# Softmax row inverses spread through DRAM instead of by GpSimd and TensorE, in the attention stage of a fused transformer layer

## The reference

```
n = (x - mean_c) / sqrt(var_c + 1e-6)                 # over channels
q, k, v = Wq n + bq, Wk n + bk, Wv n + bv             # 8 heads of 64
attn = softmax(q^T k / 8)                             # 1024 x 1024 per head
x = x + Wo (attn v) + bo
t = tokens(x);  n2 = layernorm(t)
aff = softmax(n2 gate) over 16 experts;  each expert takes its best 128 tokens of each image
t[index] += aff * (gelu(n2[index] w1 + b1) w2 + b2)
```

## Time and profile before

| | |
|---|---|
| median of 3 runs | 3368.14 us |
| range of the runs | 3366.99 to 3368.26 us |
| profiled execution, first to last instruction | 3365.4 us |
| what lies around that span | not given for the profiled execution; the median is 2.7 us above the span |
| mean granted TensorE clock | 0.976 of full speed |
| busy: PE, PEld, DVE, ACT, POOL | 3156.5, 2702.6, 2319.6, 1998.9, 1293.8 us |
| attention stage | up to about 2495 us of the span |

### The profile page before, as it was taken

How to read it: one execution, slowest core, us unless ns; L and a number is a source line. 1 busy time by engine, 2 the same in 40 slices (tenths; PEclk the granted TensorE clock), 3 DMA queues, 4 the chain that set the end, 5 groups by cost and what they waited for, 6 DMA issues and landing times. The chain is left out here.

```text
span 3365.4 us, 56592 instructions
## 1 busy us (share of the span) xinstructions
PE 3156.5 (94%) x18562; PEld 2702.6 (80%) x18562; DVE 2319.6 (69%) x3649; ACT 1998.9 (59%) x3833; POOL 1293.8 (38%) x1536
## 2 busy tenths in 40 slices
PE   6999999999999999999999999999954999999998
PEld 5988888788878887887888788888843888888886
DVE  5877587678768775875787687767756556555553
ACT  4876678478748856884787488568821333333332
POOL 1335234424523352344235233523432444444443
PEclk9999999999999999999999999999976999999999
DMA  6012111310220131113102201311132566655664
GB/s 219 26 51 104 49 51 39 113 53 26 81 97 26 51 109 45 51 40 112 53 26 95 84 26 51 113 28 37 39 114 52 139 125 139 139 135 122 150 135 59
DMA packets 108960, 269.39 MB, mean 80 GB/s; under 512 B 13456, under 2 KB 21648, under 8 KB 97936
## 3 DMA queue, kind: packets, MB, share of 16 engines
q1 hardware_dynamic: 80016, 198.80, 17.6%
q0 software_dynamic: 28672, 67.13, 11.3%
HBM read 158.40 MB, written 73.92 MB: 69 GB/s over the span
## 5 line engine op out<-in xcount | busy, mean ns | idle before, releaser
L728 DVE TENSOR_TENSOR PT<-ring,PT 128x512 fp32r<-128x512 f32 x1024 | 674.9, 686 | 226.5 <-ACT PT L476 220.1
L670 DVE TENSOR_REDUCE nmax<-S 128x1 f32<-128x1024 f32 x512 | 620.2, 1211 | 97.1 <-PE S L835 80.6
L878 PE MATMUL O<-PT,V 128*128 128x256 f32 x4096 | 677.1, 290 | 0.0
L396 POOL TENSOR_SCALAR rinv_bc<-ones,rinv 128x128 f32<-128x128 f32 x512 | 302.8, 603 | 950.3 <-DVE rinv L736 950.0
L846 PE MATMUL ring<-ident,prob 128*128 128x128 f32 x4096 | 623.3, 276 | 31.6 <-DVE qs L663 17.6
L476 ACT ACTIVATE PT<-ring 128x512 fp32r<-128x512 f32 x1024 | 581.6, 597 | 92.5 <-PE ring L846 79.8
L835 PE MATMUL S<-kd,qs 128*128 128x512 f32 x2048 | 600.2, 417 | 20.4 <-issue 17.9
L467 ACT ACTIVATE prob<-S,nmax 128x1024 f32<-128x1024 f32 x512 | 571.7, 1117 | 66.2 <-DVE nmax L670 66.2
L878 PEld LDWEIGHTS O<-PT,V 128*128 128x128 f32 x4096 | 577.4, 189 | 39.0
L846 PEld LDWEIGHTS ring<-ident,prob 128*128 128x128 f32 x4096 | 467.5, 141 | 72.0 <-DVE PT L728 31.6
L835 PEld LDWEIGHTS S<-kd,qs 128*128 128x128 f32 x2048 | 352.3, 191 | 72.6 <-issue 20.8
(11 more groups left out here) (115 smaller groups left out, 3721.1 us busy)
## 6 DMA issues: line engine op xcount, KB each, us to landing
kd<-kd SPq DMA_DIRECT2D x128, 256.0 KB, 3.6
wraw<-w_dram SPq DMA_DIRECT2D x32, 1024.0 KB, 6.7
wqk<-wqk_split SPq DMA_DIRECT2D x24, 1024.0 KB, 4.8
xt<-x_dram SPq DMA_DIRECT2D x16, 1024.0 KB, 7.2
PT<-wv_split SPq DMA_DIRECT2D x7, 2048.0 KB, 8.5
oT<-x_dram SPq DMA_DIRECT2D x24, 512.0 KB, 3.6
out_dram<-oT SPq DMA_DIRECT2D x48, 256.0 KB, 8.0
n_rows<-oT SPq DMA_DIRECT2D x48, 256.0 KB, 2.4
```

Of the source, the lines that this page charges most:

```text
L396: last_bc = nc.gpsimd.tensor_scalar(rinv_bc[:, k % 2, j, :], ones[:, :], rinv[:, 2 * k + j:2 * k + j + 1], None, ALU.mult)
L670: nc.vector.tensor_reduce(nmax[:, s:s + 1], S[:, s % 2, :], AX.X, ALU.max, negate=True).then_inc(max_done, 1)
L728: nc.vector.tensor_tensor(PT[:, 1, here[0], here[1], here[2]], ring[:, k % 2, :].rearrange("p (m q) -> p m q", m=4), PT[:, 0, here[0], her ...
L878: last_mm = nc.tensor.matmul(O[:, m % 2, 0:QC], V[:, t, head // 2, 2 * (head % 2):2 * (head % 2) + 2, :].rearrange("p h d -> p (h d)"), PT ...
```

## The change

The inverse row sums no longer go through POOL and PE. SP writes the 256 inverses of a block as one row into a DRAM tensor (from a [128 partitions x 2] tile, element by element), waits for that DMA, and loads the row back, broadcast over the 64 partitions of the head, into one of four slots of `Rs`. POOL multiplies by it as before. ACT copies the whole 128-partition product in one instruction into `oHL`; POOL now copies the other half across partitions (`oS2`) before it adds. pv_done comes from the last product. The K copies and weight loads are placed between the spreads. The residual of tiles 6 and 7 is loaded after block 2 and gets its bias at block 5, the other tiles in blocks 26 to 29, so nothing of `add_bo` is left after the last block. `ones` shrinks to one column, `n2T` moves into `Rs`.

```diff
+RES_TILES = {5: [6, 7], 26: [0], 27: [1, 2], 28: [3, 4], 29: [5]}
...
+    rinv_rows = nc.dram_tensor("rinv_rows", [BLOCKS, QC], F32).ap()
...
-        tmp = sb("tmp", [P, 3, 2, QC])
...
+        Rs = sb("Rs", [P, 4, QC])
+        oHL = sb("oHL", [P, 2, QC])
+        oS2 = sb("oS2", [P, 2, QC])
...
@@ sync
-                for p in range(1, PAIRS):
-                    duplicate_k(b, p)
-                    if p < PAIRS - 1 or not last:
-                        sp.wait_ge(ring_filled, b * RING + ring_proj(p, 3) + 1)
-                        load_pair(p % (PAIRS - 1) + 1)
...
-                for k in range(2):
+                def load_residual(k):
+                    if k == 3:
+                        sp.dma_start(spare[:, :, :], src[:, 6:8, :]).then_inc(res_in[k], 16)
+                        return
                     sp.wait_ge(os_lo, b * PIECES + 2 * k + 2)
-                    sp.dma_start(dst[:, k, :, :], src[:, 2 * k:2 * k + 2, :]).then_inc(res_in[0], 16)
...
+                    sp.sem_inc(sp_passed, 1)
+                    sp.dma_start(dst[:, k, :, :], src[:, 2 * k:2 * k + 2, :]).then_inc(res_in[k], 16)
+
+                def spread_inverse(m):
+                    row = rinv_rows[m:m + 1, :]
+                    odd = m // QB % 2
+                    sp.wait_ge(rinv_done, b * BLOCKS + m + 1)
+                    sp.dma_start(row.rearrange("a (u p) -> p (a u)", p=P), rinv[:, 2 * m:2 * m + 2],
+                                 allow_slow_non_contiguous=True).then_inc(rinv_out, 16)
+                    sp.wait_ge(rinv_out, b * (16 * BLOCKS) + 16 * m + 16)
+                    sp.sem_inc(sp_passed, 1)
+                    if m >= 4:
+                        sp.wait_ge(o_norm, b * BLOCKS + m - 3)
+                    sp.dma_start(Rs[D * odd:D * odd + D, m % 4, :], row.broadcast_to([D, QC])
+                                 ).then_inc(Rs_in[m % 4], 16)
+
+                for m in range(BLOCKS):
+                    if m % NT == NT - 1 and m < BLOCKS - 1:
+                        p = m // NT + 1
+                        duplicate_k(b, p)
+                        if p < PAIRS - 1 or not last:
+                            sp.wait_ge(ring_filled, b * RING + ring_proj(p, 3) + 1)
+                            load_pair(p % (PAIRS - 1) + 1)
+                    spread_inverse(m)
+                    if m == 2:
+                        load_residual(3)
+                    if m in (26, 27, 29):
+                        load_residual((26, 27, 29).index(m))
...
@@ gpsimd
-                        for j in range(2):
-                            last_bc = nc.gpsimd.tensor_scalar(rinv_bc[:, k % 2, j, :], ones[:, :],
-                                                              rinv[:, 2 * k + j:2 * k + j + 1], None, ALU.mult)
-                        last_bc.then_inc(rbc_done, 1)
...
-                        if BLOCKS - 2 <= k < BLOCKS:
-                            for i in range(2):
-                                add_bo(2 * (k - BLOCKS + 2) + i)
-                for i in range(4, NT):
-                    add_bo(i)
...
+                for m in range(BLOCKS):
+                    pair, odd, q = m // NT, m // QB % 2, m % QB
+                    rows, other = slice(D * odd, D * odd + D), slice(D * (1 - odd), D * (1 - odd) + D)
...
+                    for i in RES_TILES.get(m, []):
+                        add_bo(i)
...
+                    pool.wait_ge(o_copied, b * BLOCKS + m + 1)
+                    pool.sem_inc(pool_passed, 1)
+                    nc.gpsimd.tensor_copy(oS2[rows, m % 2, :], oHL[other, m % 2, :]).then_inc(o_shift, 1)
+                    pool.wait_ge(o_shift, b * BLOCKS + m + 1)
+                    nc.gpsimd.tensor_tensor(oHL[rows, m % 2, :], oHL[rows, m % 2, :], oS2[rows, m % 2, :],
+                                            ALU.add).then_inc(o_sum, 1)
+                    pool.wait_ge(o_sum, b * BLOCKS + m + 1)
+                    pool.wait_ge(Rs_in[m % 4], b * (4 * BLOCKS) + 16 * (m // 4) + 16)
+                    nc.gpsimd.tensor_tensor(oT[rows, pair, q * QC:(q + 1) * QC], oHL[rows, m % 2, :],
+                                            Rs[rows, m % 4, :], ALU.mult).then_inc(o_norm, 1)
...
@@ scalar, copy_output
-                    nc.scalar.activation(Rs[rows, m % 2, :], O[rows, m % 2, QC:2 * QC], ACT.Copy)
-                    nc.scalar.activation(oH[rows, m % 2, :], O[rows, m % 2, 0:QC], ACT.Copy)
-                    nc.scalar.activation(oL[rows, m % 2, :], O[other, m % 2, 0:QC], ACT.Copy).then_inc(o_copied, 1)
+                    nc.scalar.activation(oHL[:, m % 2, :], O[:, m % 2, 0:QC], ACT.Copy).then_inc(o_copied, 1)
...
@@ vector, tile_t
-                    dve.wait_ge(xbo, b * NT + i + 1)
+                    dve.wait_ge(xbo, b * NT + (2 if i >= 6 else i + 3))
...
@@ tensor
-                        last_mm.then_inc(pv_read, 1)
-
-                def inverse_sums(m):
-
-                    pe.wait_ge(rbc_done, b * BLOCKS + m + 1)
-                    for j in range(2):
-                        last_t = nc.tensor.transpose(O[:, m % 2, QC + j * P:QC + (j + 1) * P],
-                                                     rinv_bc[:, m % 2, j, :], ident)
-                    last_t.then_inc(pv_done, 1)
+                        last_mm.then_inc(pv_done, 1)
```

More of the change, by code:

```diff
@@ L120, in attention @@
         affT = oT[0:E, KC - 1, :]
-        tmp = sb("tmp", [P, 3, 2, QC])
[L122 to L126, removed]
+        Rs = sb("Rs", [P, 4, QC])
+        oHL = sb("oHL", [P, 2, QC])
+        oS2 = sb("oS2", [P, 2, QC])
+        n2T = Rs[:, :, :].rearrange("p (a b) c -> p a (b c)", a=2).rearrange("p a (k t) -> p a k t", k=KC)
         bv_bc = sb("bv_bc", [P, C])
@@ L133, in attention @@
         rinv = sb("rinv", [P, UNITS])
-        ones = sb("ones", [P, P])
-        rinv_bc = sb("rinv_bc", [P, 2, 2, P])
+        ones = sb("ones", [P, 1])
         stats = sb("stats", [P, 2, NT, 6])
@@ L168, in attention @@
         x_in = [sem(f"x_in{i}") for i in range(2)]
-        res_in = [sem(f"res_in{i}") for i in range(2)]
+        res_in = [sem(f"res_in{i}") for i in range(4)]
+        rinv_out = sem("rinv_out")
+        Rs_in = [sem(f"Rs_in{i}") for i in range(4)]
         wv_in = sem("wv_in")
@@ L196, in attention @@
         rinv_done = sem("rinv_done")
-        rbc_done = sem("rbc_done")
-        pv_read = sem("pv_read")
         pv_done = sem("pv_done")
         o_copied = sem("o_copied")
+        o_shift = sem("o_shift")
         o_sum = sem("o_sum")
@@ L382, in add_bo @@
                 def add_bo(i):
-                    if i % 4 == 0:
-                        pool.wait_ge(res_in[i // 4], b * 32 + 32)
+                    pool.wait_ge(res_in[i // 2], b * 16 + 16)
                     nc.gpsimd.tensor_tensor(res(i), res(i), bo_bc[:, :], ALU.add).then_inc(xbo, 1)
[L387 to L393, removed]
-                        pool.sem_inc(pool_passed, 1)
-                        for j in range(2):
-                            last_bc = nc.gpsimd.tensor_scalar(rinv_bc[:, k % 2, j, :], ones[:, :],
-                                                              rinv[:, 2 * k + j:2 * k + j + 1], None, ALU.mult)
-                        last_bc.then_inc(rbc_done, 1)
[L399 to L420, removed]
-                        if BLOCKS - 2 <= k < BLOCKS:
-                            for i in range(2):
-                                add_bo(2 * (k - BLOCKS + 2) + i)
@@ L424, in image, with tiles_added, pieces_split @@
-                for i in range(4, NT):
-                    add_bo(i)
+                def tiles_added(m):
+                    return sum(len(v) for k, v in RES_TILES.items() if k <= m)
+                def pieces_split(m):
+                    return sum(k - 2 < m for k in EARLY_BLOCK) + max(0, m - (BLOCKS - QB))
+                for m in range(BLOCKS):
+                    pair, odd, q = m // NT, m // QB % 2, m % QB
+                    rows, other = slice(D * odd, D * odd + D), slice(D * (1 - odd), D * (1 - odd) + D)
+                    if m:
+                        pool.wait_ge(o_norm, b * BLOCKS + m)
+                        pool.sem_inc(pool_passed, 1)
+                    for i in RES_TILES.get(m, []):
+                        add_bo(i)
+                    if m in RES_TILES:
+                        pool.wait_ge(xbo, b * NT + tiles_added(m))
+                        pool.sem_inc(pool_passed, 1)
+                    if pieces_split(m):
+                        pool.wait_ge(os_lo, b * PIECES + pieces_split(m))
+                        pool.sem_inc(pool_passed, 1)
+                    pool.wait_ge(o_copied, b * BLOCKS + m + 1)
+                    pool.sem_inc(pool_passed, 1)
+                    nc.gpsimd.tensor_copy(oS2[rows, m % 2, :], oHL[other, m % 2, :]).then_inc(o_shift, 1)
[6 more added lines that the diff above has]
+                                            Rs[rows, m % 4, :], ALU.mult).then_inc(o_norm, 1)
+                    for j in range(EARLY):
```

(9 more changed lines are left out.)

8 lines of the change are left out of this document (removed).

## The result

| | before | after |
|---|---|---|
| median of the runs | 3368.20 us (4 runs, 3366.99 to 3368.76) | 4386.78 us (4 runs, 4379.89 to 4393.22) |
| profiled execution, its span | 3365.4 us | 4393.22 us, span 4391.4 us |
| mean granted TensorE clock | 0.976 | 0.861 |

The ratio is 1.302 (95% interval 1.3007 to 1.3038): 1019 us slower, where 99 us faster was forecast. The range of 3225 to 3335 doesn't hold it.

The account below looks back on a forecast made before the run. The prediction took a normal block (5.68 us) to be bound by PE's rate alone. Inverse transposes 51, ACT copies 20 and residual 28 us made 99 us off 3368, so 3269 us, range 3225 to 3335.

Parts of the forecast that it names:

- SP and the DMAs at nothing: SP's write and read of the inverses: 3.0 us of SP a block, landing after 5.2, so costing nothing.
- the point that decides: In rival A: time from reciprocal to landing, r = 6.4 us, from which late inverses decide the kernel's time.
- rival A: DRAM round trip of the inverses too slow: at r = 8, 134 us more, 3403 us; chance 0.08.
- the cover: Inverses needed at POOL's product 13.2 us after their reciprocal; landing after 5.2 leaves 8 us of cover.
- Inverse transposes off PE: PE, 29 of 32 blocks: 0.22 us less each, block 5.47 us, 51 us over 8 images.
- Two ACT copies: ACT's output copies: two of three dropped, 0.68 us a block, worth 20 us (12.8 to 31.6), in the last pair.
- the chain there: Last pair, ACT to DVE to PE's next transpose: block falls from 6.14 to 5.46 us, just reaching PE's rate.
- Residual into the last pair: Wrap between images: normalisations of x no longer slowed by POOL's additions, 3.5 us a wrap, 28 us in all.
- POOL: nothing: POOL's new copy taken at 0.74 us, 2.2 us a block in all, plus late additions: costs nothing.
- B: Another chain between PE, ACT and DVE holds the block at 5.68 us: 3320 us; chance 0.12.
- C: PE not at its rate, 0.34 us a block hidden waiting: block 5.09 us, kernel 3183 us; chance 0.05.
- D: POOL's additions or the end of the last pair keep 3 to 5 us an image: about 3304 us; chance 0.15.

Follow-up runs that it names:

- probe: Separate program, no computation: SP issues seven forms of DMA one at a time; the change's write of 256 4-byte elements takes 8.35 us.
- probe2: Separate program, no computation, six forms differing in piece size, spacing or target: 256 4-byte pieces take 7.83 us adjacent, 1.57 us 64 bytes apart.
- k_on_act: Changed kernel with the K copies of pairs 1 to 3 issued by ACT instead of SP: 4216.81 us.
- old_spread: Changed kernel with the inverses again over POOL and PE; one ACT copy, POOL's shift and early residual stay: 3317.10 us, ratio 0.9845 to the kernel before.
- no_spread: Changed kernel without its two DMAs per block, the output multiplied by a tile of ones instead of the inverses: 3260.31 us.
- pair8: Changed kernel with each partition writing its two inverses as one 8-byte piece, POOL reading with a step of two: 3275.51 us, ratio 0.9724 to the kernel before.
- pipe: Changed kernel, 4-byte writes kept, SP issuing the write of a block before the read of the block before it: 3367.19 us.

## Why the prediction was wrong

**The failed step: SP and the DMAs at nothing.** The text read: "None in the trace writes single elements. The nearest for size is `affinities`, 64 KB in 2.2 us". It took 2.2, so 3.0 us of SP a block, "because most blocks have no large load in front of them". Measured: 9.6 us of SP a block, 8.2 of them at the wait for the write. The 9.1 us of the earlier trace rows was named as the upper end and comes close to the right price, though by chance: it belongs to a load of 2 KB behind large loads. It was given only to blocks with a large load ahead; `probe` shows 8.35 with nothing else running. The two rows said something of size and nothing of form. With 2.2 and 9.1 as ends and the point that decides, 6.4, between them, both sides of it needed a large chance. The Trainium skill (DMA: Bandwidth & Descriptors, Rules for kernel authors) was quoted in rival A against this write, as a non-contiguous last dim that becomes one descriptor per element. The warning pointed to the right DMA, and the packet counts agree with one descriptor per piece; but their number isn't the price, since 256 separate elements take 1.57 us in `probe2` when each has 64 bytes of its own.

**Rival A was the mechanism, with a chance of 0.08 and too small a price.** SP does one spread at a time, lags behind by 7 x (9.6 - 5.45) = 29 us in a pair, and the cover is used up. The rival had one r for two things, SP's time for a spread (9.6) and the time from reciprocal to landing (9.1 and a read of 3.9, 13 us). Even with r at 9.6 its sum gives 28.9 + 9.6 - 13.2 - 8.3 = 17 us a pair and 544 us in all, half of what was lost. Its sum let "8.3 of that" be absorbed before ACT's copy, for 134 us at r = 8. But the K copies stand in the same queue and have no such cover: PE needs them for the next pair's first scores. The prediction named that ("SP is also the queue for the K copies") and priced it for a spread of 3 us only. At 9.6 us the lag and the last spread come to 38 us, and 33 of them land on PE at each of 24 boundaries, 799 in all; the last blocks of the image and the wraps have 293 of the other 330, and there the lag of the last pair is the likely reason. `k_on_act` shows that it isn't the K queue alone: without it the inverses themselves stop ACT and PE, and 957 us are left.

**Inverse transposes off PE: right.** The block became 5.45 (forecast 5.47), PE without a wait in it. 57 us between `old_spread` and `no_spread` against 51: about 12 of them are in the wraps, which the forecast left out, and 42 in the blocks.

**Two ACT copies: not in the place forecast, and in size partly by luck.** 18 us (10 to 21) against 20. The last pair fell from 6.15 to 5.69, PE's rate in that kernel, as the chain there said, for 14 us; but the forecast had nothing elsewhere, where 15 us came, and nothing lost in the wrap, where 6 went.

**Residual into the last pair: right.** 31 to 34 us against 28, 4.0 us a wrap against 3.5. In `pair8` the normalisations of x take 0.61 each. PE's stop is 1.59 us, where it was 3.54 and below 1 was forecast, and the twelve matmuls behind it run at full speed (3.01 against 4.58):

```profile
1486.85 3.67 DVE L646 TENSOR_SCALAR xt<-xt,mv,rstd 128x512 f32<-128x512 f32 x6
...
1491.18 0.66 PE L817 MATMUL ring<-ident,xt 128*128 128x128 f32 x4 [1.59 <-DVE nT L652]
...
1491.59 3.01 PE L920 MATMUL S<-wo,nT 128*128 128x512 f32 x12
```

**POOL: nothing, right.** Its shift (L431) takes 0.39 us, where 0.74 was taken and nothing to 1.5 were the ends; additions in blocks 26 to 29 delayed no block.

**Rivals B, C and D** didn't happen: the block moved with PE's rate (5.45, not 5.68 and not 5.09), and no late block stretched. C's rule, to judge TensorE by the busy share of weight loads (the Trainium skill, Trainium Kernel Development and Optimization, Performance Expectations), would have seen 0.34 us of slack in a block of 5.68. `no_spread` has the same 0.34 in a block of 5.45 (5.11 of 5.45), with ACT 0.6 us less busy (4.74 against 5.33), so it was no slack that a quicker ACT could close.

## What to carry to other kernels

A DMA that sits in a loop with a wait behind it is priced by its form, not by its bytes: if the trace has no DMA that writes single elements, measure that one alone before the sum is made, and if its two nearest rows lie on either side of the point that decides, say so in the chances. When one queue serves two purposes, ask what each item behind the slow one has for cover, since the shortest cover sets the price. And when elements have to be scattered into DRAM, put those that one partition owns side by side, or each in 64 bytes of its own.

## What the runs showed of the hardware that was not expected

- Small writes that are neighbours in DRAM are slow together: 256 writes of 4 bytes took 7.8 to 8.4 us in 1 KB of DRAM and 1.57 us when each had its own 64 bytes. Half or twice the number made 7.50 and 9.33. The same 128 neighbours of 4 bytes took 1.9 into on-chip memory. A possible cause is that each must read and write back the same piece of memory. The Trainium skill (DMA: Bandwidth & Descriptors, Specifications) says that below 512 B a transfer does a read-modify-write. No run shows the mechanism itself, and the 512 B don't show here either: elements 64 bytes apart took no longer (1.57) than elements 512 bytes apart (1.56), and neither did pieces of 16 bytes, four to 64 bytes (1.56).
- These 8 us are mostly latency: in `pipe` such writes went out every 5.5 us without holding up the normal blocks.
- A stop of 33 us costs more than 33: the granted clock was 0.63 on average over the 46 us around it, so for some 34 of them, (1 - 0.63) x 46 / 0.5, it stood at the lower level (1.2 GHz) and not at 2.4, and the next eight matmuls of 512 columns took 3.78 us instead of 2.0.
